# Six row buffers, gathers without unit waits, and table look-ups from tile 4 in a recommendation kernel

## What is computed

```python
emb = embed_table[f_ix, x_idx]                      # (2048, 26, 16)
lin1 = w1_table[f_ix, x_idx].sum(axis=1) + w1_bias  # first-order column
fm = 0.5 * ((s * s).sum(-1) - (emb * emb).sum(...)) # s = emb.sum(axis=1)
mlp = relu(relu(h @ mlp_w1 + mlp_b1) @ mlp_w2 + mlp_b2) @ mlp_w3 + mlp_b3   # h = emb as (2048, 416)
for W in (cin_w0, cin_w1, cin_w2):                  # three interaction layers, each summed over d
    last = einsum('ndl,ndf,klf->ndk', last, x0, W); feats.append(last)
out = lin1 + fm + mlp + concat(feats).sum(axis=1) @ lin_w + lin_b
```

## Time and profile before

| | us |
|---|---|
| timed runs, median of 3 | 512.84 |
| timed runs, lowest to highest | 511.73 to 513.11 |
| profiled execution: span from the first to the last instruction | 694.2 |
| busy in the profiled execution: PE | 510.3 |
| DVE | 412.8 |
| ACT | 389.0 |
| POOL | 356.6 |

### The profile page before, as it was taken

How to read it: one execution, slowest core, us unless ns; L and a number is a source line. 1 busy time by engine, 2 the same in 40 slices (tenths; PEclk the granted TensorE clock), 3 DMA queues, 4 the chain that set the end, 5 groups by cost and what they waited for, 6 DMA issues and landing times.

```text
span 694.2 us, 6825 instructions
## 1 busy us (share of the span) xinstructions
PE 510.3 (74%) x2235; PEld 415.1 (60%) x2235; DVE 412.8 (59%) x680; ACT 389.0 (56%) x759; POOL 356.6 (51%) x365
## 2 busy tenths in 40 slices
PE   2897918824696959588695959596886949599988
PEld 2865705723484838476574747475765737478666
DVE  6431227903475748376584847484765848478866
ACT  0321628604464847376574847484665748378875
POOL 6665666774465464637466454547374664510000
PEclk9995666975896979979798989899797979899999
DMA  8836434221111111202111111112021111100000
GB/s 176 163 21 117 88 62 103 7 7 5 5 6 7 4 6 4 7 4 8 5 6 5 5 6 6 6 4 8 3 9 5 6 5 5 6 3 1 0 1 0
DMA packets 21508, 15.57 MB, mean 22 GB/s; under 512 B 12790, under 2 KB 19811, under 8 KB 21347
## 3 DMA queue, kind: packets, MB, share of 16 engines
q0 software_dynamic: 11520, 3.16, 13.5%
q1 hardware_dynamic: 6949, 9.99, 5.9%
q10 hardware_dynamic: 3005, 2.01, 1.4%
HBM read 14.92 MB, written 0.21 MB: 22 GB/s over the span
## 4 chain that ended last, share of the span: by engine, by line
PE 28%; DVE 24%; another core or an unknown queue 18%; ACT 15%; issue 11%; DMA 3%; SPq 0%; DVEq 0%
DVE z_lo L803 5%; ACT ps_s L598 5%; ACT z_hi L591 4%; PE ps_y L1197 4%; PE ps_y L1198 3%; DVE ps_y L946 3%; DVE one_hot L935 3%; PE ps_s L1097 2%; DMA w_space<-cin_w 2%; DVE sums L829 2%; PE ps_q L1111 2%; ACT room_a L597 2%; DVE ps_q L814 2%; DVE emb L950 2%
## 5 line engine op out<-in xcount | busy, mean ns | idle before, releaser
L500 POOL DMA_INDIRECT emb<-rows,idx_raw x360 | 356.3, 990 | 253.7 <-issue 101.4
L803 DVE TENSOR_TENSOR z_lo<-ps_s,z_hi 128x512 fp32r<-128x512 f32 (+1 forms) x192 | 132.1, 688 | 138.9 <-ACT ps_s L598 87.6
L591 ACT ACTIVATE z_hi<-ps_s 128x512 fp32r<-128x512 f32 (+1 forms) x192 | 114.2, 595 | 171.9 <-remote 105.6
L1197 PE MATMUL ps_y<-look_hi,one_hot 128*128 128x442 f32 x224 | 92.6, 413 | 91.4 <-DVE one_hot L935 89.6
L598 ACT ACTIVATE ps_s<-ps_s 128x512 f32<-128x512 f32 (+1 forms) x192 | 113.5, 591 | 0.7
L1111 PE MATMUL ps_q<-z_lo,zw_hi 128*127 128x512 f32 (+1 forms) x192 | 86.9, 453 | 32.6 <-DVE z_lo L803 21.1
L1197 PEld LDWEIGHTS ps_y<-look_hi,one_hot 128*128 128x128 f32 x224 | 49.5, 221 | 101.0 <-DVE emb L950 57.1
L1198 PE MATMUL ps_y<-look_lo,one_hot 128*128 128x442 f32 x224 | 89.3, 400 | 0.0
L946 DVE SCALAR_TENSOR_TENSOR ps_y<-tables,look_place,ps_y 128x442 f32<-128x442 f32 x56 | 37.9, 677 | 78.6 <-remote 70.6
L1097 PE MATMUL ps_s<-xt,pick 128*128 128x512 f32 (+1 forms) x192 | 77.1, 414 | 8.6 <-ACT x L582 5.4
L1113 PE MATMUL ps_q<-z_hi,zw_hi 128*127 128x512 f32 (+1 forms) x192 | 78.9, 411 | 0.0
(11 more groups left out here) (191 smaller groups left out, 765.0 us busy)
## 6 DMA issues: line engine op xcount, KB each, us to landing
emb<-rows,idx_raw POOLq DMA_INDIRECT x360
w_space<-rows SPq DMA_DIRECT2D x2, 728.9 KB
m_space<-rows SPq DMA_DIRECT2D x2, 728.9 KB
w_space<-key_scratch SPq DMA_DIRECT2D x1, 1408.0 KB
w<-cin_w SPq DMA_DIRECT2D x2, 416.0 KB, 4.8
w<-cin_w ACTq DMA_DIRECT2D x2, 416.0 KB, 7.6
w_space<-cin_w SPq DMA_DIRECT2D x2, 416.0 KB
w_space<-cin_w ACTq DMA_DIRECT2D x2, 416.0 KB
```

What stands on the lines that cost most here:

```text
L500: pool.indirect_dma_start(emb[t % EMB][:, f, :], None, rows, bass.IndirectOffsetOnAxis(row_ix[:, t, f:f + 1], 0)).then_inc(gathered[t] if ...
L591: act.activation(z_hi[0:k, c, :], ps[0:k, :], ACT.Square)
L803: z = dve.tensor_tensor(z_lo[0:k, u % NC, :], ps, z_hi[0:k, u % NC, :].bitcast(F32), ALU.subtract)
L1197: pe.matmul(o, one_hot[n % 2][:, j, :], look_hi[i][:, ws], start=(j == 0), stop=False)
```

## The change

The row buffers become six. The waits of POOL for units are removed, so that after the setup a gather waits only for its buffer. Look-ups begin with tile 4, so that tiles 2 and 3 gather all 26 fields, and look_at is shifted by two tiles so that the look-ups keep their distance. The splits of the tables are spread: the first in tile 0, the second and third in tile 1, the fourth in tile 2.

```diff
-FIRST_LOOK = 2
+FIRST_LOOK = 4
+AHEAD = 2
 LATER = 2
 EARLY = 18
-PER_UNIT = 2
...
-        EMB = 3
+        EMB = 6
...
         def look_at(t, slot):
 
-            n = LOOKS * t + slot - LATER
+            n = LOOKS * (t - FIRST_LOOK + AHEAD) + slot - LATER
             return (FIRST_LOOK + n // LOOKS, n % LOOKS) if 0 <= n < look_no(T, 0) else None
 
         def looked_by(t):
 
-            return min(max(LOOKS * t + 1 - LATER, 0), look_no(T, 0))
+            return min(max(LOOKS * (t - FIRST_LOOK + AHEAD) + 1 - LATER, 0), look_no(T, 0))
 
-        LOOK_SPLIT = {3: 0, 5: 1, 7: 2, 9: 3}
+        LOOK_SPLIT = {(0, 5): 0, (1, 3): 1, (1, 8): 2, (2, 3): 3}
...
-                    if t >= EMB - 1 and f and f % PER_UNIT == 0:
-                        behind = s_no(t - EMB, NC + f // PER_UNIT - 1) if t >= EMB else s_no(0, f // PER_UNIT)
-                        pool.wait_ge(hi_ready, behind + 1)
...
-                    if t == 0 and u in LOOK_SPLIT:
-                        look_high(LOOK_SPLIT[u])
+                    if (t, u) in LOOK_SPLIT:
+                        look_high(LOOK_SPLIT[t, u])
...
-                    if t == 0 and u - 2 in LOOK_SPLIT:
-                        look_low(LOOK_SPLIT[u - 2])
+                    if (t, u - 2) in LOOK_SPLIT:
+                        look_low(LOOK_SPLIT[t, u - 2])
```

## The result

The changed kernel takes 522.23 us (median of 4 runs, 520.94 to 523.14) against 512.29 for the kernel before, timed beside it (median of 4): ratio 1.0183, interval 1.0155 to 1.0212. It is slower by 9.9 us. The prediction said 519, slower, in a range of 506 to 524.

A forecast was written before the change was run, and what follows sets the result against it. Before, POOL's gathers and PE/DVE bound the kernel almost equally; after, POOL's gathers do. With gathers 1% cheaper untraced, 73.9 + 448.9 - 3.8 gave 519.0 us, range 506 to 524.

The forecast's parts named there:

- The two clocks: Kernel before: end times set by PE/DVE and by POOL's gathers, S + 438.9 and S + 440.1, about 1 us apart.
- Engine clock: End as set by the compute engines' tiles: S + 438.9 before, S + 433.1 after, range 430 to 436.
- S: Start of tile 0's sum of the first-order column: 80.14 in the trace, solved as 72.7 or 73.9 for timed runs.
- the three tiles: Tiles 0 to 2 with the splits spread and fewer look-ups: together 81.2 us against 87.3 before.
- Nobody reads it before tile 3, so nothing: Load of the remaining keys, leaving a tile later because it waits for the second split: no cost.
- Gather clock: End as set by POOL's gathers, one every 1.25 us: S + 440.1 before, S + 448.9 after.
- The choice of 1% off: Assumed 1% tracing overhead on a gather: forecast 519.0 us, taken over 521.6 at exactly 1.25 us a gather.
- Late tiles: ACT's copies wait for gathers at tiles 2 to 4; tile 3's rows 5.7 us late, tile 4's 8.2.
- Blocked gathers: POOL gathers held beside DVE work: 13 us in the queue to tile 14; 8 fewer masks give back 1.2.
- Engines stay the bound: Rival: untraced gathers cost clearly less, POOL is on time, 507 us, range 504 to 511; chance 0.29.
- The pauses are real: Rival: engines stand still beside gathers in timed runs, 24 us over seven unpaced tiles, about 530; chance 0.07.
- It cancels: Rival: at a period of 1.20 to 1.22 us, late tiles 3 and 4 offset saved look-ups, 511.5 to 514.5; chance 0.11.

The follow-up runs named there:

- experiments 2 and 3: Kernel before with six buffers and no unit waits: 512.15 us; changed kernel with three buffers and the unit waits back: 522.19 us.
- experiment 4: Kernel before plus 8 gathers into a buffer that nobody reads, four each after tile 2's and tile 3's: 522.58 us, ratio 1.021.
- experiment 7: Changed kernel without its 8 added gathers and without those of fields 20 and 21 in tiles 6 to 15: 506.3 us, ratio 0.9901.
- experiment 6: Kernel before without the 20 gathers of fields 20 and 21 in tiles 6 to 15: 511.49 us, ratio 0.9995.
- experiment 11: Changed kernel with look-ups from tile 3 (364 gathers), splits moved, and no POOL waits in the setup: 511.89 us, ratio 1.0005.

## Why the prediction was right, step by step

**The two clocks.** Reading the disturbed profile by taking the gap-free tile of 27.39 from the earlier trace rows and the gather of 0.947 + 0.30 from the earlier trace rows was right: the undisturbed profile has ten tiles of 27.38 to 27.41 and the same gather. The look of slack in the earlier trace rows, 78.0 and 57.1 us, was an effect of the long tiles alone; experiments 2 and 3 show that buffers and unit waits cost nothing. That the added gathers are the loss is shown by experiment 4, and experiment 7 shows that the rest of the change costs nothing.

**Engine clock.** Forecast S + 438.9; experiment 6, which has no late gather, gives 510.1 - 67.8 = S + 442.3. The difference is tile 0: I took 32.5, it is 35.7. After: forecast S + 433.1 (the three tiles, 81.2 for 87.3, would give 432.8), experiment 7 gives 503.7 - 66.1 = S + 437.6. So the saving, put at 5.8, is 4.7, or 7.5 without the 2.8 that tile 2's rows landed late. "Nobody reads it before tile 3, so nothing" was said of the later load of the keys; experiment 7 suggests that it has this other price.

**Gather clock.** The step that failed in size is where the queue starts. I took gather 42 at S - 8.8 from the earlier trace rows, where it had waited 4.45 us for by_row_done. Undisturbed, POOL waits for no setup step after index 22, and from gather 23 on the queue never stops:

```profile
38.10 0.95 POOL L497 DMA_INDIRECT emb<-rows,idx_raw  x1 [2.69 <-PE ps_q L1032]
```

Gather 42 starts at 61.86, S - 3.6, and at S - 4.3 in the kernel before. Counted from 38.10, tile 14's last gather is 323 periods on: 38.1 + 403.8 + 0.95 + 12.0 blocked + 3.0 to land (the page's median) = 457.8, where its copy stands, and 63.1 more is the end. The tail was forecast as 63.9 minus 1.0.

**Why the total came near all the same.** From the start of tile 0 the undisturbed profiles give S + 444.1 before and S + 455.4 after, where I had 440.1 and 448.9. I also set the sum equal to the timed run, which is 1.8 us longer than its span. These misses did little harm because S was no measurement: I solved it from the time of before, 72.7, where it is 67.0, and so it took up 5.7 us of them in before and after alike. That is a calibration, and what was predicted with it is the difference: 8.8 us at the traced price, measured 9.9.

**The choice of 1% off.** Of two sums I took 519.0, with a gather 1% cheaper outside a profile, and not 521.6 at the traced price. No row gave this 1%. It is the term that puts the forecast 3.2 us below the result: the loss so forecast is 6.2 us, the measured one 9.9. Eight gathers more cost 10.8 us in timed runs (experiment 4), so the traced price was right. That the setup would have to be shorter (S = 72.7) spoke against it then; it is shorter still, 65.5 to 68.7 in the undisturbed profiles.

**Late tiles.** Tiles 2 to 4 were named as waiting, tile 3 with 5.7 and tile 4 with 8.2 us; measured waits of the copies are 4.60 and 8.86 for tiles 2 and 3, and tile 4 then is nearly on time (0.1) because tile 3 has waited. The mechanism was right and came one tile earlier than priced, as a queue that starts 5.2 us later against the engines would make it.

**Blocked gathers.** After 38 us the surplus over 0.947 is 339.7 - 346 x 0.947 = 12.0 us, near the 13 forecast. I had said that the low halves block gathers as the Trainium skill's rule has it and the masks in the trace do not. That reading was wrong; the masks do it too. The Trainium skill (SBUF — State Buffer, "Who interferes with whom") says that a DVE instruction with two SBUF inputs contends with a GpSimd instruction that reads SBUF, and that the one that issues first holds the shared ports until it ends. The undisturbed profile agrees:

```profile
157.69 0.68 DVE L932 TENSOR_TENSOR one_hot<-key_first,tables 128x512 fp32r<-128x512 f16 x1
...
157.78 1.43 POOL L497 DMA_INDIRECT emb<-rows,idx_raw  x1 [0.30 <-issue]
```

The gather starts 0.09 us after the mask and ends 0.82 after the mask's end. So it is with all 20 gathers that a mask stretches, to 1.02 to 1.47 us, and with those that the tables' low halves stretch: the gather ends 0.82 us after the DVE instruction does. Where the gather had started before the mask, or at most 0.03 us after it, it took its usual 0.95; in the six cases with 0.01 to 0.03 us it was the mask that took longer, 0.73 to 0.76 instead of 0.68. A price for each mask is therefore an average over the places where it falls, 6.6 us for 48 masks or 0.14 each here, near the 0.15 assumed; 0.68 for each would be far too much.

**Rivals.** "Engines stay the bound" did not happen, but experiment 7 shows that its gain exists. "The pauses are real" fell with the undisturbed profiles. "It cancels" had asked for a period of 1.20 to 1.22 us, which no run has; experiment 11 does come out level, but with four gathers fewer and an earlier queue.

## What to carry to other kernels

When a profile is much longer than the timed runs, look for a stretch of the same work without the gaps, build the time from it, and compare every engine's fixed cost per round with that shorter round: an engine that seems to wait for a third of the time may be full. Where work is shifted from a shared load (look-ups on PE and DVE) to a serial queue (gathers on POOL), price it in the queue, and ask at which tile the queue is first late: later slack does not bring back what waits there. A busy share of 70% with a constant gap behind each instruction was here a saturated engine. And before a late arrival is put down to a queue, compare its time from issue to landing with the median: in experiment 7 the rows were issued in time.

## What the runs showed of the hardware that was not expected

The same program, profiled twice, spanned 694.2 and 511.1 us. In the longer one tiles with gathers took 38.1 us and more and the first without them 27.4, at nearly equal durations of the DVE and ACT instructions: PE, DVE and ACT stood still together for 4.0 to 6.2 us in most of them. What caused it stays open and was not tried.

An indirect gather of 128 rows of 68 bytes cost 0.944 to 0.947 us (medians) and 0.30 behind it in all profiles, in the setup under heavy loads as in the loop, except where a DVE instruction held it. From its issue to its landing it took 3.0 us (median), where I had assumed 2. Beside the 1152 KB load of the keys the changed kernel's gathers took up to 7.2 us to land. A low half of 1.88 us on DVE had stretched that one to 2.25 on POOL; the next, of the usual length, took 6.7.
